# Two routed adapters on one core: weights fetched in one transfer and a step earlier, and two groups of weight factors moved in VectorE's order

## The chip, the cores and the metric

One core of one Trainium2 chip. The metric is the device time of one execution in microseconds (us); lower is better. Engines are named as in the profile: PE is TensorE, DVE VectorE, ACT ScalarE, POOL GpSimd, SP SyncE (here it only issues DMAs).

## The reference

128 items of 128 rows by 1024 columns pass two layers. Each layer is an adapter, and each item is routed to one of three sets of its weights (the drawn routes are 1 and 2, so two sets are used in each layer).

```
h = gelu(x @ W_down[route] + b_down[route])      # 1024 -> 512
y = x + h @ W_up[route] + b_up[route]            # 512 -> 1024
out = (y - mean) * rsqrt(var + 1e-5) * gamma[route] + beta[route]
```

Everything is fp32. The second layer takes the first one's output.

## The kernel before

**Order of the work.** The items are sorted on the chip by route and taken in pairs: 65 pairs for layer 0, 65 for layer 1, numbered 0 to 129. A pair takes one set of weights. Where the set of pair c differs from that of pair c-1, the flag `c_new[c]` is 1. It is 1 at the first pair and at three more, which the trace places at pairs 30, 65 (the change of layer) and 95. `c_near` marks new sets whose forerunner came one or two pairs before, `c_far` the others. All engines read these flags in branches written by `when` (load the flag from memory into a register, compare, jump over the body).

**Precision.** Each fp32 operand is split in a high part (ACT copies it to fp32r) and a low part (DVE subtracts the high one), and each product is three matmuls. So a new set of down weights costs ACT four copies (`high_wd`, L578) and DVE four subtractions (`low_wd`, L797), each of 128x1024. The up projection is done with seven products of blocks instead of eight, so a new set of up weights gives seven factors: three DVE operations form differences (`factors`, L822 to L826), a fourth follows (L835), and each of the seven factors takes an ACT copy (L593) and a DVE subtraction (`low_wu`, L816). Factors 0 to 3 are made in `take_wu_0`, 4 to 6 in `take_wu_2`.

**A step.** In step i PE does the down projection of pair i (two items, four quarters each, six matmuls per quarter, `down`, L506) interleaved with the seven products of pair i-3 (`product`, L518): 48 + 42 = 90 matmuls. The order is product 0, a quarter, product 1, a quarter, and so on, with the two last quarters after product 6. Products 0, 2, 4 and 6 go to a bank bX, 1, 3 and 5 to bZ. After a product DVE adds the bank to the rows in memory before PE may add to that bank again: `onto` (evictions 1 to 3, L901) and `last_onto` (4 to 7, L909). PE waits for eviction 3 before product 4 and for eviction 4 before product 5. ACT seeds the banks with biases (`seed_x` L651, `seed_z` L659), which must be there before product 0 and product 1 of the next step, and which wait for DVE's sign `s_cb`. `high_x`, `low_x` make the parts of the input, `high_h`, `low_h` (L674, L891) those of the hidden layer; `low_h(w, 0)` is the first group of them, `low_h(w, 1)` the second, and so on. In layer 1 DVE also transposes the input (L862), twice in a step. `square` (L684), `normal` (L692) on ACT, `scale` (L932) on DVE and `shift` (L452) on POOL are the layer norm.

**Order on DVE and ACT.** Each engine runs `end(i-1)`, then `begin(i)`, in that order, in loops of six steps; the jump back lies between `begin` of one step and its `end`. Those loops end their turns in steps 10, 16, 22 ... 58 and 75, 81 ... 123. On DVE `begin(i)` finishes with `low_h(w, 0)`, `take_wu_2` under its flag, the sign `s_wu[1]` that lets product 4 go, and `factors` under `c_near`. Then `end(i)` begins with eviction 3, the variance, two `scale`, `low_h(w, 1)` and eviction 4.

**Weights.** `fetch_down` asks for a set with eight DMAs of 256 KB, `fetch_up` likewise. For pair i+1 ACT issues `fetch_down` in `begin(i)` (`load_down`), half a step before the first use in `end(i)`; for the up weights two steps before. The first down weights and up weights are issued by SP.

## Time and profile before

| | |
|---|---|
| median of three runs | 2795.27 us (2795.16 to 2796.49) |
| time of the profiled execution | 2799.51 us |
| span of that execution, first to last instruction | 2797.6 us |
| granted TensorE clock, mean | 0.988 |
| PE / DVE / ACT / POOL busy | 96% / 74% / 60% / 49% of the span |
| DMA queue of SP / of ACT | 557.02 MB / 12.59 MB |

The busy time of PE counts matmuls whose ends are modelled and which overlap, so it isn't PE at its peak. The starts of matmuls are the better measure, and the rows below use them.

### The profile page before, as it was taken

How to read it: one execution, taken by the hardware profiler on the slowest of the kernel's cores; microseconds unless marked ns; L12 is line 12 of the kernel's file. 1: busy time of each engine (PE TensorE's matmuls, PEld its weight loads, DVE VectorE, ACT ScalarE, POOL GpSimd, SP SyncE). 2: the span in 40 equal slices, each digit the busy share in tenths (PEclk: the TensorE clock that was granted, in tenths of full speed). 3: DMA queues.
4: the chain of work that ended last, by engine and by line, in shares of the span. 5: the costliest groups of instructions: out<-in, count | busy, mean ns of one | idle time of the engine just before them, and what ended most of it. 6: DMA issues, size and time to landing. Idle time of an engine off the chain costs nothing.

```text
span 2797.6 us, 58384 instructions
## 1 busy us (share of the span) xinstructions
PE 2697.8 (96%) x11714; PEld 2209.0 (79%) x11714; DVE 2074.1 (74%) x3356; ACT 1676.1 (60%) x2905; POOL 1369.0 (49%) x1050
## 2 busy tenths in 40 slices
PE   7999999998999999999989999999889999999997
PEld 5788888877788888888768888888667888888885
DVE  5767677768777676777788777777787777877776
ACT  4565665655666656666556665656556656666564
POOL 1455555544455555555435444444434444544445
PEclk9999999999999999999999999999999999999999
DMA  7665566667565665656856665766766666666663
GB/s 197 202 214 201 204 212 199 212 208 219 192 210 199 214 203 201 213 204 208 240 184 222 200 212 188 223 197 219 206 205 208 205 207 201 209 198 218 203 202 146
DMA packets 366252, 574.00 MB, mean 205 GB/s; under 512 B 40992, under 2 KB 240800, under 8 KB 365728
## 3 DMA queue, kind: packets, MB, share of 16 engines
q1 hardware_dynamic: 360352, 557.02, 60.9%
q10 hardware_dynamic: 5376, 12.59, 1.9%
q14 instruction: 512, 4.19, 0.5%
q8 instruction: 12, 0.20, 0.0%
HBM read 364.97 MB, written 204.47 MB: 204 GB/s over the span
## 4 chain that ended last, share of the span: by engine, by line
PE 78%; issue 8%; DVE 7%; DVEq 2%; ACT 2%; DMA 1%; ACTq 1%; POOL 1%; SPq 0%; POOLq 0%
PE pD L506 41%; PE bX L518 21%; PE bZ L518 16%; DVEq L234 2%; DVE xt L909 1%; DVE hl L891 1%; DVE xt L932 1%; DMA rwd<-in_Wd 1%; DVE wul L816 1%; ACT xh L626 1%; ACTq L234 1%; DVE xT L862 0%; ACT pC L684 0%; DMA htok<-hg 0%; DVE xt L901 0%
## 5 line engine op out<-in xcount | busy, mean ns | idle before, releaser
L452 POOL TENSOR_TENSOR xt<-xt,cgb 128x1024 f32<-128x1024 f32 x258 | 621.1, 2408 | 455.3 <-ACT xt L692 455.3
L506 PE MATMUL pD<-wdh,xh 128*128 128x512 f32 x2080 | 814.1, 391 | 10.0 <-DVEq L853 9.6
L506 PE MATMUL pD<-wdl,xh 128*128 128x512 f32 x2080 | 812.1, 390 | 0.0
L506 PE MATMUL pD<-wdh,xl 128*128 128x512 f32 x2080 | 811.6, 390 | 0.0
L692 ACT ACTIVATE xt<-xt,rstd 128x1024 f32<-128x1024 f32 x258 | 296.1, 1148 | 297.0 <-POOL rstd L438 293.6
L506 PEld LDWEIGHTS pD<-wdh,xh 128*128 128x128 f32 x2080 | 392.7, 189 | 95.9 <-DVEq L853 8.4
L518 PE MATMUL bX<-wuh,hh 128*128 128x512 f32 x1040 | 411.0, 395 | 51.1 <-DVE xt L901 26.5
L684 ACT ACTIVATE pC<-xt,nmean 128x512 f32<-128x512 f32 x520 | 358.2, 689 | 169.0 <-DVE nmean L917 160.4
L506 PEld LDWEIGHTS pD<-wdl,xh 128*128 128x128 f32 x2080 | 392.9, 189 | 81.5
L506 PEld LDWEIGHTS pD<-wdh,xl 128*128 128x128 f32 x2080 | 392.3, 189 | 82.3
L674 ACT ACTIVATE hh<-cs 128x512 fp32r<-128x512 f32 x260 | 163.7, 630 | 465.3 <-PE bX L518 221.1
L518 PE MATMUL bX<-wul,hh 128*128 128x512 f32 x1040 | 408.1, 392 | 0.0
L518 PE MATMUL bX<-wuh,hl 128*128 128x512 f32 x1040 | 408.1, 392 | 0.0
L460 POOL TENSOR_TENSOR cs<-hT 128x256 f32<-128x256 f32 x130 | 96.9, 745 | 597.0 <-DVE hT L876 597.0
L435 POOL TENSOR_TENSOR rstd<-var,mhalf 128x2 f32<-128x2 f32 x129 | 215.3, 1669 | 348.8 <-DVE var L924 346.2
L891 DVE TENSOR_TENSOR hl<-cs,hh 128x512 fp32r<-128x512 f32 x260 | 191.0, 735 | 235.9 <-issue 208.4
L901 DVE TENSOR_TENSOR xt<-bX,xt 128x512 f32<-128x512 f32 x260 | 178.1, 685 | 240.9 <-PE bX L518 126.3
L518 PE MATMUL bZ<-wuh,hh 128*128 128x512 f32 x780 | 307.8, 395 | 21.0 <-DVE xt L909 16.1
L932 DVE SCALAR_TENSOR_TENSOR xt<-xt,nmean,cgb 128x1024 f32<-128x1024 f32 x260 | 321.8, 1278 | 0.6 <-POOLq L472 0.6
L518 PE MATMUL bZ<-wul,hh 128*128 128x512 f32 x780 | 304.7, 391 | 0.0
L518 PE MATMUL bZ<-wuh,hl 128*128 128x512 f32 x780 | 304.6, 391 | 0.0
L518 PEld LDWEIGHTS bX<-wuh,hh 128*128 128x128 f32 x1040 | 196.9, 189 | 100.9 <-DVE xt L901 33.7
(104 smaller groups left out, 3837.8 us busy)
## 6 DMA issues: line engine op xcount, KB each, us to landing
xq<-in_xB SPq DMA_DIRECT2D x130, 512.0 KB, 3.5
htok<-hg SPq DMA_DIRECT2D x260, 256.0 KB, 2.8
hq<-htok SPq DMA_DIRECT2D x1040, 64.0 KB, 2.2
xt<-in_x SPq DMA_DIRECT2D x130, 512.0 KB, 4.2
mid<-xt SPq DMA_DIRECT2D x130, 512.0 KB, 3.4
xq<-mid SPq DMA_DIRECT2D x520, 128.0 KB, 3.2
xt<-mid SPq DMA_DIRECT2D x130, 512.0 KB, 4.0
out<-xt SPq DMA_DIRECT2D x128, 512.0 KB, 2.9
```

The lines of the kernel that those rows point to most:

```text
L234: with eng.If(eng.value_load(flags[0:1, bass.ds(p.times(1), 1)], min_val=0, max_val=1) == 1):
L435: eng.tensor_tensor(rstd[:, n:n + 2], var[:, n:n + 2], mhalf[:, 0:1].broadcast_to([128, 2]), ALU.pow)\
L452: eng.tensor_tensor(xt[:, k, :], xt[:, k, :], cgb[:, 1, :], ALU.add).then_inc(s_o, 1)
L460: eng.tensor_tensor(cs[:, 0, :], b1, b2, ALU.add).then_inc(s_S, 1)
L506: last = eng.matmul(pD[e][:, :], a[:, e, 128 * k:128 * k + 128], w[:, k, :], start=False, stop=(k == 7 and n == 2), skip_group_check=True)
L518: last = eng.matmul(bank[:, :], a[:, left, 128 * c:128 * c + 128], w[:, n, c, :], start=(start and c == 0 and m == 0), stop=(c == 1 and m ...
L674: eng.activation(dst, src, ACT.Copy).then_inc(s_hh, 1)
L684: eng.activation(junk[:, :], xt[:, u.slot(e), K * m:K * m + K], ACT.Square, bias=nmean[:, n:n + 1], accum_out=ssq[:, b, m, e:e + 1]).then_ ...
L692: eng.activation(xt[:, k, :], xt[:, k, :], ACT.Copy, scale=rstd[:, n:n + 1]).then_inc(s_z, 1)
L891: eng.tensor_tensor(blocks, src, high.bitcast(fp32), ALU.subtract).then_inc(s_hl, 1)
L901: eng.tensor_tensor(half(u, e, m), bank[:, :], half(u, e, m), ALU.add).then_inc(s_v, 1)
L932: eng.scalar_tensor_tensor(out=xt[:, k, :], in0=xt[:, k, :], scalar=nmean[:, n:n + 1], in1=cgb[:, 0, :], op0=ALU.add, op1=ALU.mult).then_i ...
```

## The change

1. The host lays the weights out as they lie on chip, so that one partition's part is one contiguous run (16 KB). `fetch_down` and `fetch_up` are then one DMA of 2 MB each. Only the very first down weights come in four DMAs of 512 KB, one for each quarter, with a semaphore each.
2. The down weights are asked for one step further ahead: at a far new set in `begin` two steps before, at a near one as before. After `high_h(w, 0)` ACT then has five flagged branches in a step where it had four.
3. The first up weights are issued by ACT in `begin(0)` instead of by SP in its step 0.
4. On DVE `take_wu_2` (factors 4 to 6), its sign and the near `factors` branch move from ahead of eviction 3 to behind it.
5. On DVE `take_wu_0` (factors 0 to 3) and the signs `s_cb`, `s_wu[0]` move from ahead of eviction 6 to behind eviction 6 and `mean(u, 0, 6)`. In it the subtraction on the bias `cbu` (L837) moves from the end to the front.

```
         def fetch_down(eng, row, c):
             eng.wait_ge(f_rd, c + 1)
-            for h in range(2):
-                for a in range(4):
-                    r = 256 * a + 128 * h
-                    eng.dma_start(rwd[32 * a:32 * a + 32, 4 * h:4 * h + 4, :],
-                                  Wd[row, r:r + 128, :].rearrange("a (k i) n -> (a i) k n", i=32)).then_inc(s_rd[h], 16)
+            eng.dma_start(rwd[:, :, :].rearrange("p k n -> p (k n)"), Wd[row, :, :].rearrange("a p n -> (a p) n"))\
+               .then_inc(s_rd, 16)
...
# SP, before its steps
-            fetch_down(eng, row, 0)
+            eng.wait_ge(f_rd, 1)
+            for q in range(4):
+                eng.dma_start(rwd[:, 2 * q:2 * q + 2, :].rearrange("p k n -> p (k n)"),
+                              Wd[row, :, 2 * K * q:2 * K * q + 2 * K].rearrange("a p n -> (a p) n")).then_inc(s_rd0[q], 16)
...
# SP, step(i)
-                if i.first():
-                    fetch_up(eng, adapter(i), 0)
...
# ACT, begin(i)
                 high_h(i + -2, 0)
+                if i.first():
+                    fetch_up(eng, adapter(i), 0)
                 when_new(eng, i + -3, take_wu_2)
...
                 when(eng, c_near, i + -2, load_up)
                 when(eng, c_far, i, load_up)
-                when(eng, c_new, i + 1, load_down)
+                when(eng, c_near, i + 1, load_down)
+                when(eng, c_far, i + 2, load_down)
...
# DVE, take_wu_0
+                eng.wait_ge(s_bu, c * 16 + 16)
+                eng.tensor_tensor(cbu[:, K:H], cbu[:, K:H], cbu[:, 0:K], ALU.subtract).then_inc(s_bz, 1)
                 low_wu(c * 7, 0, b11)
...
                 eng.tensor_tensor(b11, t2, b11, ALU.subtract).then_inc(s_sub, 1)
-                eng.wait_ge(s_bu, c * 16 + 16)
-                eng.tensor_tensor(cbu[:, K:H], cbu[:, K:H], cbu[:, 0:K], ALU.subtract).then_inc(s_bz, 1)
...
# DVE, begin(i)
                 low_h(w, 0)
-                when_new(eng, u, take_wu_2)
-                ready(u, s_wu[1])
...
-                when(eng, c_near, w, factors)
...
# DVE, end(i)
                 onto(u, 3, X, 0, 1)
+                when_new(eng, u, take_wu_2)
+                ready(u, s_wu[1])
+                when(eng, c_near, w, factors)
...
                 low_x(i + 1, 0)
-                when(eng, c_new, w, take_wu_0)
-                ready(w, s_wu[0])
-                ready(w, s_cb)
                 last_onto(u, 6, bZ, 0, 0, 1)
                 mean(u, 0, 6)
+                when(eng, c_new, w, take_wu_0)
+                ready(w, s_cb)
+                ready(w, s_wu[0])
                 transpose_x(i + 1, 1)
```

## Rows read from the trace of the kernel before

**Rows 1.** The page's first part: busy time, share, instructions.

```profile
PE 2697.8 (96%) x11714; PEld 2209.0 (79%) x11714; DVE 2074.1 (74%) x3356; ACT 1676.1 (60%) x2905; POOL 1369.0 (49%) x1050
```

**Rows 2.** Timeline of PE (start, length, work, idle before): the starts of steps.

```profile
598.52 0.39 PE L518 MATMUL bX<-wuh,hh 128*128 128x512 f32 x1
...
627.51 0.80 PE L518 MATMUL bX<-wuh,hh 128*128 128x512 f32 x1 [2.56 <-ACT bX L651]
...
701.08 0.77 PE L518 MATMUL bX<-wuh,hh 128*128 128x512 f32 x1 [5.77 <-ACT bX L651]
...
750.00 0.39 PE L518 MATMUL bX<-wuh,hh 128*128 128x512 f32 x1
...
1364.24 0.40 PE L518 MATMUL bX<-wuh,hh 128*128 128x512 f32 x1
...
1465.79 0.39 PE L518 MATMUL bX<-wuh,hh 128*128 128x512 f32 x1
...
1979.70 0.39 PE L518 MATMUL bX<-wuh,hh 128*128 128x512 f32 x1
...
2005.54 0.47 PE L518 MATMUL bX<-wuh,hh 128*128 128x512 f32 x1 [0.85 <-issue]
...
2130.53 0.39 PE L518 MATMUL bX<-wuh,hh 128*128 128x512 f32 x1
```

**Rows 3.** Windows of the core: PE, PEld, DVE, ACT, POOL busy, clock, DMA.

```profile
616.20:620.50 4.30, 4.28 (x12) 3.36 (x13) 3.98 (x6) 1.63 (x3) 2.14 (x1) 0.60 1.03 227
...
1465.80:1588.20 122.40, 122.40 (x542) 101.39 (x541) 97.26 (x161) 76.50 (x136) 60.21 (x49) 1.00 0.67 219
```

**Rows 4.** Timeline of ACT and PE in step 29, ahead of pair 30.

```profile
607.78 6.24 ACTq L262 DMA_DIRECT2D rwd<-in_Wd  x8
...
616.23 0.50 PE L518 MATMUL bZ<-wuh,hh 128*128 128x512 f32 x1 [3.94 <-DVE xt L909]
...
623.40 2.01 ACT L578 ACTIVATE wdh<-rwd 128x1024 fp32r<-128x1024 f32 x2 [5.58 <-DMA rwd<-in_Wd]
```

**Rows 5.** Timeline of the start (ACT, SP, PE).

```profile
16.62 2.00 ACT L578 ACTIVATE wdh<-rwd 128x1024 fp32r<-128x1024 f32 x2 [1.00 <-DMA rwd<-in_Wd]
...
27.56 4.27 SPq L270 DMA_DIRECT2D rwu<-in_Wu  x8
...
51.17 0.50 PE L506 MATMUL pD<-wdh,xh 128*128 128x512 f32 x1 [2.53 <-DVEq L853]
```

**Rows 6.** Timeline of DVE: eviction 3 in steps 29 and 81.

```profile
606.50 0.69 DVE L901 TENSOR_TENSOR xt<-bX,xt 128x512 f32<-128x512 f32 x1 [1.47 <-issue]
...
1721.84 0.69 DVE L901 TENSOR_TENSOR xt<-bX,xt 128x512 f32<-128x512 f32 x1 [4.58 <-PE bZ L518]
```

**Rows 7.** Timeline of DVE and PE, layer 1: eviction 4, product 5 (steps 70, 81).

```profile
1517.26 0.68 DVE L909 SCALAR_TENSOR_TENSOR xt<-bZ,xt 128x512 f32<-128x512 f32 x1
...
1520.19 0.39 PE L518 MATMUL bZ<-wuh,hh 128*128 128x512 f32 x1
...
1726.26 0.50 PE L518 MATMUL bZ<-wuh,hh 128*128 128x512 f32 x1 [0.54 <-DVE xt L909]
```

**Rows 8.** Timeline of PE in step 67, behind `factors` of pair 65.

```profile
1414.84 0.50 PE L506 MATMUL pD<-wdh,xh 128*128 128x512 f32 x1 [1.48 <-DVEq L853]
```

**Rows 9.** Timeline of DVE in step 32: factors 0 to 3 of pair 30.

```profile
691.59 2.35 DVE L816 TENSOR_TENSOR wul<-rwu,wuh 128x1024 fp32r<-128x1024 f32 x2
...
696.13 3.36 DVE L835 TENSOR_TENSOR rwu<-twu,rwu 128x1024 f32<-128x1024 f32 x1
...
700.53 0.69 DVE L909 SCALAR_TENSOR_TENSOR xt<-bZ,xt 128x512 f32<-128x512 f32 x1 [0.43 <-DVE cbu L837]
```

**Rows 10.** Timeline of DVE and PE in step 33: factors 4 to 6 of pair 30, and eviction 3.

```profile
710.43 2.96 DVE L816 TENSOR_TENSOR wul<-rwu,wuh 128x1024 fp32r<-128x1024 f32 x2 [0.40 <-ACT wuh L593]
...
715.75 0.69 DVE L901 TENSOR_TENSOR xt<-bX,xt 128x512 f32<-128x512 f32 x1 [1.22 <-issue]
...
716.50 0.50 PE L518 MATMUL bX<-wuh,hh 128*128 128x512 f32 x1 [2.17 <-DVE xt L901]
```

More of the change, by code:

```diff
@@ L106, in routed_adapters @@
         c_first = sb("c_first", [1, 1], i32)
-        c_q = sb("c_q", [1, NPH + 1], i32)
+        c_q = sb("c_q", [1, NPH + 2], i32)
         c_new = sb("c_new", [1, NPH + 1], i32)
-        c_near = sb("c_near", [1, NPH], i32)
-        c_far = sb("c_far", [1, NPH], i32)
+        c_near = sb("c_near", [1, NPH + 2], i32)
+        c_far = sb("c_far", [1, NPH + 2], i32)
         rf, tf, kf, rq = (xt[:, 0, (NB + 1) * n:(NB + 1) * (n + 1)] for n in range(4))
@@ L132, in routed_adapters @@
             "s_it", "s_io", "s_id", "s_p", "s_first", "s_oh", "s_pc", "s_ctl", "s_far"))
-        s_rd = [sem(f"s_rd{k}") for k in range(2)]
+        s_rd0 = [sem(f"s_rd0{k}") for k in range(4)]
+        s_rd = sem("s_rd")
         s_ru = sem("s_ru")
@@ L258, in fetch_down @@
             eng.wait_ge(f_rd, c + 1)
-            for h in range(2):
-                for a in range(4):
-                    r = 256 * a + 128 * h
-                    eng.dma_start(rwd[32 * a:32 * a + 32, 4 * h:4 * h + 4, :],
-                                  Wd[row, r:r + 128, :].rearrange("a (k i) n -> (a i) k n", i=32)).then_inc(s_rd[h], 16)
+            eng.dma_start(rwd[:, :, :].rearrange("p k n -> p (k n)"), Wd[row, :, :].rearrange("a p n -> (a p) n"))\
+               .then_inc(s_rd, 16)
         def fetch_up(eng, row, c):
             eng.wait_ge(f_ru, c + 1)
-            for g in range(2):
-                for a in range(4):
-                    r = 128 * a + 64 * g
-                    eng.dma_start(rwu[32 * a:32 * a + 32, g, :, :, :].rearrange("p c n k -> p c (n k)"),
-                                  Wu[row, r:r + 64, :].rearrange("a (k i) n -> (a i) k n", i=32)).then_inc(s_ru, 16)
+            eng.dma_start(rwu[:, :, :, :, :].rearrange("p g c n k -> p (g c n k)"),
+                          Wu[row, :, :].rearrange("a p n -> (a p) n")).then_inc(s_ru, 16)
         b11, b12, b21, b22 = (rwu[:, g, :, n, :] for g in range(2) for n in range(2))
@@ L576, in high_wd @@
                 count(eng, s_Db, p + -1, 4, q + 1)
-                eng.wait_ge(s_rd[q // 2], c * 64 + 64)
+                if p.first():
+                    eng.wait_ge(s_rd0[q], 16)
+                else:
+                    eng.wait_ge(s_rd, c * 16)
                 eng.activation(wdh[:, 2 * q:2 * q + 2, :], rwd[:, 2 * q:2 * q + 2, :], ACT.Copy).then_inc(s_wdh, 1)
@@ L597, in take_wu_0 @@
                 count(eng, s_P, p + -1, 7, 4)
-                eng.wait_ge(s_ru, c * 128 + 128)
+                eng.wait_ge(s_ru, c * 16 + 16)
                 high_wu(0, b11)
@@ L784, in _ @@
             eng.memset(c_near[:, 0:1], 0)
+            eng.memset(c_near[:, NPH:NPH + 2], 0)
+            eng.memset(c_far[:, NPH:NPH + 2], 0)
             eng.tensor_tensor(c_near[:, 1:2], c_new[:, 1:2], c_new[:, 0:1], ALU.min)
@@ L1023 @@
         "itok": itok_B_1_2,
-        "Wd": np.concatenate([L0_cond_W_down, L1_cond_W_down]),
+        "Wd": np.concatenate([L0_cond_W_down, L1_cond_W_down]).reshape(6, 4, 8, 32, K).transpose(0, 1, 3, 2, 4)
+                .reshape(6, 128, 8 * K),
         "bd": np.concatenate([L0_cond_b_down, L1_cond_b_down]),
-        "Wu": np.concatenate([L0_cond_W_up, L1_cond_W_up]),
+        "Wu": np.concatenate([L0_cond_W_up, L1_cond_W_up]).reshape(6, 4, 4, 32, H).transpose(0, 1, 3, 2, 4)
+                .reshape(6, 128, 4 * H),
         "bu": np.concatenate([L0_cond_b_up, L1_cond_b_up]),
```

4 lines of the change are left out of this document (2 added, 2 removed).

## The prediction

> **What bounds the kernel now.** The page's first part comes first [rows 1]: PE is busy 96%, so the end is set by PE's stream wherever that runs, and a gain must come from its holes. How long a step is without one, a window shows: 122.40 us hold 542 matmuls, six steps of 90, so 20.40 a step at a clock of 1.00, the 2.4 GHz level [rows 3]. 130 such steps would be 2652; the span is 2797.6. Then the timeline of PE: the reader should lay step starts beside each other and take 20.40 off for each step between. Around pair 30 the six steps 29 to 34 take 151.48, 29.1 too much. Around pair 65 the four steps 65 to 68 take 101.55, 20.0 too much. Around pair 95 the six steps 94 to 99 take 150.83, 28.4 too much [rows 2]. That is 77.5 us at three new sets of weights. The rest is the start, the tail, and a hole of 0.2 to 1.4 us in most of the eighteen steps in which DVE's and ACT's loops turn; the last row of [rows 7] is one. In a plain step DVE, ACT and POOL lie beside PE, so an operation saved there gains nothing.
>
> **Part 1, weights in one DMA and a step ahead.** In step 29 eight DMAs hold ACT for 6.24; its `high_h(w, 1)` comes after them, DVE's eviction 4 behind that, and product 5 waits 3.94 [rows 4]. The pause costs clock too: from 616.20 to 620.50 the granted clock is 0.60, mostly the 1.2 GHz level [rows 3], and some nine matmuls come 0.2 late each. Then ACT waits 5.58 for the weights [rows 4], and step 30 starts 2.56 late for its bias seed [rows 2]. Step 29 lasts 28.99, 8.6 too much. Both waits go. The DMA now issued in step 28 costs ACT an eighth of 6.24, 0.8; nothing is queued there but `high_h(w, 1)`, which had some 1.4 to spare. With one more branch (0.9, below) that cover is just used up, and I leave 0.9 in steps 28 and 29: gain 7.7, bounds 6.5 and 8.6. Step 94 is the same case at 25.84, 5.4 too much [rows 2]; DVE enters step 95 with more in front of it (part 4), for which I give 0.8 back: gain 4.6, bounds 3 and 5.4. For pair 65 the weights arrive in time already; the up weights' eight DMAs on ACT delay an eviction slightly: gain 0.3. Steps 30, 65 and 95 stay long: four copies on ACT (two in 2.01 [rows 4]) and four subtractions on DVE lie ahead of eviction 1. The new wait for the buffer two steps ahead is long met at a far set.
>
> The Trainium skill, DMA: Bandwidth & Descriptors, section Queues, rings and completion order, says that each DMA engine alternates between queues a whole packet at a time, of up to 64 descriptors. By that rule rows of 16 KB could hold other transfers back behind much of the 2 MB. No row here has such a transfer; what it would do is rival (d), priced from rows.
>
> **Part 2, the start.** ACT waits 1.00 for half of the first weights [rows 5]. A first quarter lands sooner: gain 1.0, bounds 0 and 1.0. The first up weights are issued by SP for 4.27 from 27.56, and the `htok` and `hq` transfers run beside them; PE then waits 2.53 at 51.17, where DVE had to wait for `hq` [rows 5]. ACT can issue the one DMA at about 25, ahead of nothing that is due, and SP's queue loses eight, so the jam ends 3 to 6 earlier. I take this wait and 0.5 of a smaller one: gain 3.0, bounds 0 (the bytes are as slow) and 5.
>
> **Part 3, two branches behind eviction 3.** Between `low_h(w, 0)` (0.41) and eviction 3 the sequencer of DVE takes the two untaken branches: 0.41 + 1.47 idle [rows 6], some 0.9 a branch where no instruction runs over it. Behind eviction 3 (0.69) 0.6 of them is covered. In a plain step eviction 3 waits for PE anyway, so what follows it comes 1.15 later. The cover is the slack of eviction 4: in layer 1 it ends at 1517.94, product 5 goes at 1520.19 [rows 7], 2.25 to spare. So nothing is lost while the delay is below 2.25. In a turning step DVE is what PE waits for (4.58 idle for branches and the jump [rows 6]), and the 0.6 is a gain, capped by the hole. In layer 0 eight such steps give 3.8, step 34 another 0.6: gain 4.4, bounds 0 and 5.4.
>
> **Part 4, the third branch, in layer 1.** The `take_wu_0` branch is covered by `low_x` now. Behind the mean (0.2) some 0.75 of it is bare. In layer 0 DVE's waits for PE take that up. In layer 1 two transposes fill DVE: 1.15 and the bare branch, less what an eviction's wait gives, make 1.6 by the end of a step, and a wait of 0.5 ahead of eviction 2 leaves 1.1 at `low_h(w, 0)`. Less the 0.6 of part 3, nine turning steps have 0.5 more hole: loss 4.5, bounds 0 and 9.
>
> **Part 5, `factors`.** In steps 31, 66 and 96 it stands behind the same branch, and the sign for the next quarter of `down` stands behind it; in step 67 PE already waits 1.48 for that [rows 8], so every delay counts. 0.85, 1.3 and 1.3: loss 3.4, bounds 0 and 5.
>
> **Part 6, factors 0 to 3.** In step 32 DVE starts them at 691.59 and is at eviction 6 at 700.53, 3.36 of it in one subtraction [rows 9]; the seed of step 33 is late by 5.77 [rows 2]. Now they start behind product 5 (692.6), eviction 6 (0.69), the mean and a branch, at about 694.2: 2.6 later, and `s_cb` with them. The bias subtraction in front adds no wait, as the bias is asked for at that step's start; queued behind it are the four subtractions. In steps 67 and 97 DVE waited for ACT's copy anyway: 0.9 each. Loss 4.4, bounds 1 and 8.
>
> The Trainium skill, SBUF — State Buffer, section SBUF: two separate sides, has POOL and DVE shut each other out for a whole instruction where both read that memory and DVE has two inputs. The 3.36 agrees, as other subtractions take 1.2. By that rule the wait only moves to another subtraction; without it the sum would be some 6 lower.
>
> **Part 7, factors 4 to 6.** In step 33 three subtractions run from 710.43, then a branch, then eviction 3 at 715.75, for which PE waits 2.17 [rows 10]. Now eviction 3 goes at 710.3, a branch, the subtractions end at 715.3, and the second branch is hidden: 1.0 sooner. By the same count 0 in step 68, 0.7 in 98, 1.8 in step 3: gain 3.5, bounds 0 and 5.
>
> **Sum.** -7.7 - 4.6 - 0.3 - 1.0 - 3.0 - 4.4 - 3.5 + 4.5 + 3.4 + 4.4 = -12.2, and 0.3 back in step 65, whose DVE work starts later: -11.9. The profiled execution took 2799.51, 1.9 over its span and 4.2 over the median of the three runs; the difference is taken off the median: 2795.27 - 11.9 = 2783.4.
>
> **The rivals.** (a) The forecast, 2783.4: 0.46. With the parts' bounds (not all at one end) its own range is 2775 to 2790.
>
> (b) The moved work costs nothing. From 691 to 720 DVE is busy throughout, and its sum is the same in either order, so the 12.3 of losses go: 2795.3 - 24.2 = 2771, or 2775 with a third of them left. Against it: the bare branch. 0.16.
>
> (c) It doesn't do what it is made for. Steps 29 and 94 keep half of their 14.0, since DVE's and ACT's own work holds them: 2783.4 + 7 - 1 = 2789 or, with the start's 4.0 gone too, 2793. For it: the steps behind new down weights are long even at pair 65, where the weights come in time. Against it: the 3.94 and the 5.58 have one cause each. 0.15.
>
> (d) The 2 MB crowds SP's transfers. At the 219 to 227 GB/s of [rows 3] it lasts some 9 us; a `htok` store behind all of it eats the time until the transposes, and PE is held 2 to 4 at some of six fetches: 8 in all, 2791. For it: the wait at 51.17. Against it: the loads now start early in a step, ahead of the stores. 0.09.
>
> (e) Slower: eviction 4 in the plain steps of layer 1. It decides where DVE's delay passes 2.25. If the bare branches cost twice my 1.15, or the delay of part 4 isn't taken up by the waits and adds itself, some 55 plain steps grow; at 0.3 each that is 16.5, and 5 at the turns: 2805. For it: DVE has no other slack there. Against it: the 1.47. 0.14.
>
> **How the numbers follow.** A measurement of this kernel tells 0.2%, 5.6 us, from no change, so faster is below 2789.7. Of (a) 0.43 is faster, of (b) all, of (c) and (d) 0.05: 0.64. The same: the rest of (a), (c) and (d), 0.22. Slower: (e), 0.14. The range reaches from (b) to the far end of (c), 2771 to 2798; (e) and the tails lie outside.
>
> **What would show it.** Right: steps 29 and 94 within 1.5 of 20.40 and ACT's issue one DMA long; the seed of step 33 late by about 8; holes at turns smaller in layer 0, larger in layer 1. Wrong: plain steps over 20.40, a wait for `hq` or `htok` in steps 28 to 33, the seed's wait unchanged.

## The result, and the profile after

The changed kernel took 2833.28 us (2831.68 to 2837.71, four runs), the kernel before 2795.74 beside it. The ratio is 1.0137, 95% interval 1.0119 to 1.0154: slower by about 38, where 12 faster had been forecast.

The first part of the page, to be laid beside [rows 1]:

```profile
span 2835.8 us, 58851 instructions
PE 2713.0 (96%) x11714; PEld 2216.1 (78%) x11714; DVE 2084.8 (74%) x3358; ACT 1682.4 (59%) x2905; POOL 1348.3 (48%) x1050
```

The counts and the shares tell little: PE is again "busy 96%". Its busy time grew by 15.2 of the 38, because a matmul at a slower clock counts as busy for longer (0.63 in rows below, 0.39 in [rows 2]). The fourth part, the chain that ended last, says more. First the kernel before, then the changed one:

```profile
PE 78%; issue 8%; DVE 7%; DVEq 2%; ACT 2%; DMA 1%; ACTq 1%; POOL 1%; SPq 0%; POOLq 0%
```

```profile
issue 30%; PE 24%; DVE 19%; DVEq 11%; ACT 7%; POOL 6%; ACTq 2%; POOLq 1%; DMA 0%; SPq 0%
PE pD L503 12%; DVEq L236 10%; PE bX L515 7%; PE bZ L515 5%; DVE xt L914 5%; ACT xh L626 5%; DVE hl L896 4%; POOL rstd L432 2%; DVE xT L867 2%; DVE xt L937 2%; POOL cs L459 2%; ACT pC L684 1%; DVE xt L906 1%; ACTq L236 1%; DVE wul L821 1%
```

The chain ran through PE before; now it runs through DVE and its sequencer. L236 is the branch in `when`: 10% of the span on DVE's queue, where its line in the chain of the kernel before (L234) had 2%.

**Where the 38 came.** The sum over steps, each from its first matmul of product 0 to the next step's (worked out from the timeline of PE; a step without a hole is 20.40; the stretch 130 to 132 ends with the start of the last matmul). "Turning" are the steps in which DVE's and ACT's loops turn and no new set lies near: 10, 16, 22, 40, 46, 52, 58 and 75, 81, 87, 105, 111, 117, 123. The other columns are experiments, told below.

| stretch (steps) | before | after | e1 | e13 | e3 | e4 | e5 | e9 | e12 | e10 | e14 |
|---|---|---|---|---|---|---|---|---|---|---|---|
| start of step 4 | 85.6 | 77.8 | 81.0 | 78.4 | 83.7 | 84.4 | 85.4 | 85.6 | 85.7 | 77.6 | 76.3 |
| turning, layer 0 (7) | 147.3 | 156.9 | 148.5 | 146.3 | 147.2 | 163.0 | 150.7 | 173.7 | 156.0 | 147.2 | 144.8 |
| turning, layer 1 (7) | 148.7 | 167.9 | 150.1 | 154.4 | 152.9 | 161.9 | 156.7 | 171.5 | 162.8 | 149.5 | 144.3 |
| 28 to 34 | 172.6 | 176.5 | 167.7 | 169.6 | 172.1 | 176.9 | 174.2 | 181.6 | 177.7 | 166.8 | 163.4 |
| 64 to 68 | 122.0 | 124.3 | 120.7 | 122.6 | 125.7 | 125.9 | 124.9 | 132.1 | 124.3 | 121.2 | 119.9 |
| 93 to 99 | 172.1 | 175.9 | 171.3 | 177.0 | 173.2 | 176.9 | 174.7 | 182.6 | 180.2 | 170.9 | 164.9 |
| 130 to 132 | 41.6 | 45.7 | 40.9 | 43.0 | 43.7 | 42.9 | 41.1 | 42.8 | 40.3 | 41.5 | 40.5 |
| others, layer 0 (46) | 938.4 | 940.6 | 938.4 | 938.4 | 938.4 | 946.8 | 938.4 | 959.6 | 939.2 | 938.4 | 938.4 |
| others, layer 1 (47) | 958.8 | 959.5 | 958.8 | 958.8 | 958.8 | 963.2 | 959.0 | 990.3 | 962.1 | 958.8 | 958.8 |

From before to after: -7.8 at the start, +9.6 and +19.2 at the turning steps, +3.9, +2.3 and +3.8 around the three new sets, +4.1 in the tail, +2.9 in all others: 38.0, and the spans differ by 38.2. Three quarters of the loss lie in fourteen steps that have nothing to do with weights.

**A turning step in layer 1.** Step 81 starts at 1724.97. Timeline of DVE; eviction 3 (L906, 1734.81) answers to [rows 6], eviction 4 (the last row) to [rows 7]:

```profile
1722.83 1.26 DVE L867 STREAM_TRANSPOSE xT<-xq 128x1024 f32<-128x1024 f32 x1 [1.26 <-issue]
1725.25 0.69 DVE L896 TENSOR_TENSOR hl<-cs,hh 128x512 fp32r<-128x512 f32 x1 [1.16 <-issue]
...
1731.33 0.84 DVE L896 TENSOR_TENSOR hl<-hT,hh 128x256 fp32r<-128x256 f32 x1
1734.81 0.69 DVE L906 TENSOR_TENSOR xt<-bX,xt 128x512 f32<-128x512 f32 x1 [2.64 <-PE bZ L515]
1736.86 0.16 DVE L929 SCALAR_TENSOR_TENSOR var<-ssq 128x2 f32<-128x2 f32 x1 [1.36 <-issue]
...
1740.10 0.68 DVE L914 SCALAR_TENSOR_TENSOR xt<-bZ,xt 128x512 f32<-128x512 f32 x1
```

of DVE in the kernel before, where step 81 starts at 1711.96:

```profile
1710.15 0.69 DVE L891 TENSOR_TENSOR hl<-cs,hh 128x512 fp32r<-128x512 f32 x1 [1.31 <-issue]
...
1725.52 0.68 DVE L909 SCALAR_TENSOR_TENSOR xt<-bZ,xt 128x512 f32<-128x512 f32 x1
```

and of PE after, product 5, which goes with eviction 4:

```profile
1740.83 0.58 PE L515 MATMUL bZ<-wuh,hh 128*128 128x512 f32 x1 [1.91 <-DVE xt L914]
...
1742.07 0.63 PE L515 MATMUL bZ<-wuh,hh 128*128 128x512 f32 x1
1742.50 0.63 PE L515 MATMUL bZ<-wul,hh 128*128 128x512 f32 x1
```

The reader is to see the delay being handed on. The first half of the step begins with `low_h(u, 2)` (L896) at 1725.25, 0.28 behind the step's start; in the kernel before it was at 1710.15, 1.81 ahead of it. `low_h(w, 0)` follows at 1731.33, the loop turns with no branch beside it, and eviction 3 runs at T+9.84 (T being the step's start), as early as before. But then come two branches, 1.36 bare ahead of `var`, and eviction 4 runs at T+15.13. In the kernel before it was at T+13.6. PE waits 1.91 instead of the 0.54 of [rows 7].

The rows of eviction 3 name "PE bZ", product 3, as what ended its idle time, here and in [rows 6]. By the code it waits for product 2 alone, and where it runs before product 3 has ended (T+9.24 in the kernel before, step 16) the profile names "issue". So the 4.58 of [rows 6] is indeed DVE's sequencer, as the prediction read it.

What comes behind PE's wait is slow. Windows of the changed kernel (as [rows 3]): ahead of the wait, behind it, and, for comparison, behind the wait of step 87, which is 1.91 as well:

```profile
1728.00:1735.40 7.40, 7.40 (x34) 6.12 (x33) 4.66 (x7) 2.95 (x6) 2.89 (x4) 1.00 0.54 160
1740.80:1744.50 3.70, 3.67 (x9) 2.90 (x10) 3.12 (x5) 2.44 (x4) 1.59 (x1) 0.54 0.30 120
...
1867.40:1871.10 3.70, 3.70 (x16) 3.08 (x17) 3.11 (x5) 2.47 (x4) 1.57 (x1) 1.00 0.31 123
```

Behind the pause of 0.54 the kernel before kept a clock of 1.00. Behind that of 1.91 in step 81 it is 0.54, nearly all at the 1.2 GHz level, with matmuls 0.43 apart (the last two rows above) instead of some 0.23. That is why 1.4 more of waiting makes the step 3.2 longer (21.23 and 24.41). It doesn't follow each such wait: of layer 1's seven turning steps, all with waits of 1.91 to 1.94, five lose clock and take 24.3 to 24.5, while two (87 and 105) keep it and take 23.0. In layer 0 one of seven loses it (step 16). These runs don't show what decides it. I had counted this multiplier in step 29 and nowhere else.

**Layer 0.** Step 22, the same picture with the end of the other branch. Timeline of DVE, after:

```profile
451.42 0.69 DVE L896 TENSOR_TENSOR hl<-cs,hh 128x512 fp32r<-128x512 f32 x1 [3.43 <-issue]
...
462.44 0.16 DVE L929 SCALAR_TENSOR_TENSOR var<-ssq 128x2 f32<-128x2 f32 x1 [1.37 <-issue]
```

and before:

```profile
451.65 0.69 DVE L891 TENSOR_TENSOR hl<-cs,hh 128x512 fp32r<-128x512 f32 x1 [2.15 <-issue]
```

Three branches behind the mean hold the sequencer for 3.43; two held it for 2.15. Over 43 plain steps of layer 0 (between 5 and 61) the median pause from the mean's end to this `hl` was 2.42 before and 3.83 after: **1.4 for the branch that I had put at 0.75**, with two signs, which e6 below puts at 0.1. In layer 1 this branch alone lies between the mean and the next transpose: nothing is idle there before, and the median over 42 plain steps is 1.27 after. The waits of the whole run say it in totals, the kernel before first:

```profile
DVE hl L891 <- issue: 208.4, 119, 2.5
ACT bX L651 <- DVEq L853: 17.3, 4, 5.0
PE bZ L518 <- DVE xt L909: 16.1, 20, 3.9
```

```profile
DVE hl L896 <- issue: 269.5, 120, 4.5
ACT bX L651 <- DVEq L858: 210.4, 127, 6.1
DVE var L929 <- issue: 137.6, 128, 1.4
PE bZ L515 <- DVE xt L914: 41.7, 21, 4.9
```

The second line is a sign raised late, not by itself a loss: ScalarE's bias seed now waits for DVE's sequencer in 127 steps instead of 4.

**The weights.** What the change was made for worked: step 29 took 28.99 before and 20.40 after, step 94 25.84 and 20.40. But the step in front grew: step 28 from 21.08 to 27.22, step 93 from 21.25 to 27.81, and so did the step behind, 30 from 26.69 to 28.85, 95 from 27.46 to 29.13. The three steps 28 to 30 took 76.75 before and 76.47 after, 93 to 95 took 74.54 and 77.34: nothing was gained in all. Timeline of ACT and PE in step 28, after, answering to [rows 4]:

```profile
585.02 0.35 ACTq L261 DMA_DIRECT2D rwd<-in_Wd  x1
592.03 0.63 ACT L674 ACTIVATE hh<-cs 128x512 fp32r<-128x512 f32 x1 [10.84 <-issue]
...
594.05 0.67 PE L515 MATMUL bZ<-wuh,hh 128*128 128x512 f32 x1 [4.94 <-DVE xt L914]
```

The DMA is 0.35 long, as I had said. `high_h(w, 1)` runs 7.01 behind it all the same: step 28 is one in which ACT's loop turns, and the taken branch stands right ahead of the turn. PE then waits 4.94 in that step for the eviction behind it.

**The factors.** Timeline of DVE in steps 32 and 33 and of PE in step 33, after, answering to [rows 9, 10]:

```profile
692.79 0.69 DVE L836 TENSOR_TENSOR cbu<-cbu 128x512 f32<-128x512 f32 x1 [1.19 <-issue]
...
695.67 3.36 DVE L821 TENSOR_TENSOR wul<-twu,wuh 128x1024 fp32r<-128x1024 f32 x1
...
700.09 1.21 DVE L842 TENSOR_TENSOR rwu<-twu,rwu 128x1024 f32<-128x1024 f32 x1
...
711.00 0.69 DVE L906 TENSOR_TENSOR xt<-bX,xt 128x512 f32<-128x512 f32 x1 [1.51 <-PE bX L515]
...
715.63 0.47 PE L515 MATMUL bX<-wuh,hh 128*128 128x512 f32 x1 [0.59 <-DVEq L858]
...
720.34 0.50 PE L515 MATMUL bZ<-wuh,hh 128*128 128x512 f32 x1 [1.74 <-DVE xt L914]
```

and of PE in step 33 of the kernel before, product 5, behind the product 4 of [rows 10]:

```profile
720.17 0.50 PE L518 MATMUL bZ<-wuh,hh 128*128 128x512 f32 x1 [0.61 <-DVE xt L909]
```

Eviction 3 of step 33 waits for PE alone again, and the 3.36, which stood in another subtraction [rows 9], is found in a low part instead, while the old one takes 1.21. That the wait only moves is what the prediction drew from the Trainium skill, SBUF — State Buffer, section SBUF: two separate sides; the trace agrees with its number. Product 4 comes 1.0 sooner in its step (T+14.38, before T+15.42), but the three subtractions now stand ahead of eviction 4, and product 5 waits 1.74 instead of 0.61: both kernels have it at T+19.09, and step 33 takes 26.02 in both. Step 32 takes 26.49 before and 29.03 after. The seed of step 33 came 6.47 late instead of 5.77, and PE waits 1.44 for the sign behind `factors`, for which it didn't wait before.

### The profile page after: what moved, and what is told of

Read it like the earlier page. It is cut to its first block, busy times and chain, and to the rows that moved or that the text cites. A ratio compares the mean times of both kernels' runs of the same rounds, so it can differ in the third digit from the quotient of the medians.

```text
span 2835.8 us, 58851 instructions
## 1 busy us (share of the span) xinstructions
PE 2713.0 (96%) x11714; PEld 2216.1 (78%) x11714; DVE 2084.8 (74%) x3358; ACT 1682.4 (59%) x2905; POOL 1348.3 (48%) x1050
## 3 DMA queue, kind: packets, MB, share of 16 engines
q14 instruction: 467, 3.83, 0.5%
## 4 chain that ended last, share of the span: by engine, by line
issue 30%; PE 24%; DVE 19%; DVEq 11%; ACT 7%; POOL 6%; ACTq 2%; POOLq 1%; DMA 0%; SPq 0%
PE pD L503 12%; DVEq L236 10%; PE bX L515 7%; PE bZ L515 5%; DVE xt L914 5%; ACT xh L626 5%; DVE hl L896 4%; POOL rstd L432 2%; DVE xT L867 2%; DVE xt L937 2%; POOL cs L459 2%; ACT pC L684 1%; DVE xt L906 1%; ACTq L236 1%; DVE wul L821 1%
## 5 line engine op out<-in xcount | busy, mean ns | idle before, releaser
L449 POOL TENSOR_TENSOR xt<-xt,cgb 128x1024 f32<-128x1024 f32 x258 | 629.6, 2441 | 433.9 <-ACT xt L692 433.9
L896 DVE TENSOR_TENSOR hl<-cs,hh 128x512 fp32r<-128x512 f32 x260 | 179.3, 690 | 295.8 <-issue 269.5
L432 POOL TENSOR_TENSOR rstd<-var,mhalf 128x2 f32<-128x2 f32 x129 | 186.0, 1442 | 281.3 <-DVE var L929 281.3
L874 DVE TENSOR_TENSOR xl<-xq,xh 128x1024 fp32r<-128x1024 f32 x130 | 234.8, 1806 | 39.3 <-ACT xh L626 33.2
```

The lines of the kernel that those rows point to most:

```text
L432: eng.tensor_tensor(rstd[:, n:n + 2], var[:, n:n + 2], mhalf[:, 0:1].broadcast_to([128, 2]), ALU.pow)\
L449: eng.tensor_tensor(xt[:, k, :], xt[:, k, :], cgb[:, 1, :], ALU.add).then_inc(s_o, 1)
L874: eng.tensor_tensor(xl[:, e, :], src, xh[:, e, :].bitcast(fp32), ALU.subtract).then_inc(s_xl, 1)
L896: eng.tensor_tensor(blocks, src, high.bitcast(fp32), ALU.subtract).then_inc(s_hl, 1)
```

## The experiments

Fourteen runs, in four groups that each had the kernel before on the same chip.

| run | median, us | range | ratio to before | 95% interval |
|---|---|---|---|---|
| e1 | 2789.25 | 2786.15 to 2792.43 | 0.9972 | 0.9959 to 0.9984 |
| e2 | 2847.76 | 2845.82 to 2854.3 | 1.0175 | 1.0158 to 1.0192 |
| e3 | 2810.05 | 2806.68 to 2811.77 | 1.0043 | 1.0026 to 1.006 |
| e4 | 2856.05 | 2853.5 to 2862.31 | 1.0214 | 1.0194 to 1.0233 |
| e5 | 2819.2 | 2817.52 to 2819.91 | 1.0082 | 1.0065 to 1.0098 |
| e9 | 2933.18 | 2927.53 to 2934.29 | 1.0484 | 1.0466 to 1.0501 |
| e6 | 2799.49 | 2797.41 to 2802.13 | 1.0008 | 0.9999 to 1.0018 |
| e7 | 2784.98 | 2784.07 to 2786.77 | 0.9958 | 0.9944 to 0.9972 |
| e8 | 2785.58 | 2782.88 to 2789.75 | 0.9961 | 0.9947 to 0.9974 |
| e10 | 2784.75 | 2783.78 to 2787.17 | 0.996 | 0.9944 to 0.9975 |
| e11 | 2791.53 | 2787.6 to 2794.29 | 0.998 | 0.9971 to 0.9989 |
| e12 | 2843.98 | 2840.92 to 2846.67 | 1.0173 | 1.0157 to 1.0188 |
| e13 | 2802.92 | 2800.14 to 2807.52 | 1.0025 | 1.0016 to 1.0035 |
| e14 | 2766.31 | 2763.81 to 2769.91 | 0.99 | 0.9884 to 0.9917 |

### Which half of the change: VectorE's order, or the rest

**e1**, the changed kernel with VectorE's order of before (both moves below undone):

```
             low_h(w, 0)
+            when_new(eng, u, take_wu_2)
+            ready(u, s_wu[1])
...
+            when(eng, c_near, w, factors)
...
             onto(u, 3, X, 0, 1)
-            when_new(eng, u, take_wu_2)
-            ready(u, s_wu[1])
-            when(eng, c_near, w, factors)
...
             low_x(i + 1, 0)
+            when(eng, c_new, w, take_wu_0)
+            ready(w, s_wu[0])
+            ready(w, s_cb)
             last_onto(u, 6, bZ, 0, 0, 1)
             mean(u, 0, 6)
-            when(eng, c_new, w, take_wu_0)
-            ready(w, s_cb)
-            ready(w, s_wu[0])
```

> The changed kernel with VectorE's order of before (factors 0 to 3 ahead of eviction 6, factors 4 to 6 ahead of eviction 3, the bias subtraction last); weights in one DMA, a step ahead, as changed. Theory A, untaken branches that no DVE instruction runs over make DVE late, so that PE waits for eviction 4 in the turning steps and its clock falls: those steps go back to about 21.2 us, the start's gain of 7.8 stays, and the time is about 2786 (2780 to 2791). Theory B, ACT's fifth branch in a step and its loads make high_h(w, 1) late: the turning steps stay at 22 to 24.4, about 2825. Theory C, the 2 MB transfers hold up others: 2825 or more too, with waits on hq or xq.

Measured 2789.25, with turning steps of 21.2 and 21.4, as theory A had it; the start kept 4.6 of the 7.8. The order alone turns a gain of 8 into a loss of 38. ScalarE's added branch and the wide transfers are still in this kernel, so neither costs that much by itself.

**e2**, the kernel before with both moves (the diff above with its signs turned round, and the bias subtraction ahead of the four low parts in `take_wu_0`) and nothing else; **e3**, with the two branches behind eviction 3 alone; **e4**, with the branch of `take_wu_0`, its signs and the bias subtraction behind the mean alone.

> The kernel before with both of VectorE's moves and nothing else. Theory A: all the loss of the turning steps is here, 29 us, with 4 in the tail and 5 to 10 around the new sets, so 2830 (2822 to 2840). Theories B and C: within 5 us of before, 2791 to 2801.

> The kernel before with factors 4 to 6 and the near-factors branch behind eviction 3, and nothing else. Theory A: the two branches now cost 1.35 behind eviction 3, which plain steps absorb; in a turning step they are partly covered; -3 to +4 in all, 2796 (2791 to 2801). If the number of branches between eviction 3 and eviction 4 is what counts by itself, PE waits some 1.3 us more in 18 turning steps: 2819 or more.

> The kernel before with factors 0 to 3 behind eviction 6 and the mean, the bias subtraction first, and nothing else. Theory A: one bare branch of 1.2, which reaches low_h(w, 0) with 0.5 to 0.7 left and is paid in 18 turning steps (some 11), in three factor steps (3.6) and at the seeds of three new sets (4): 2813 (2805 to 2822). If this move is harmless: within 3 us of before.

Measured: 2847.76, 2810.05 and 2856.05, each above theory A's range (e3 lies between its two accounts). That the loss lies in VectorE's order alone was right, and every size was too low: e3 costs 13, where about nothing was expected, e4 59, both together 51. In e4 DVE reaches `low_h(u, 2)` of step 22 0.77 behind the step's start, `hl` waiting 3.44 for issue, and is late for eviction 3 (T+12.3, before T+10.3) and eviction 4 alike; putting the other two branches behind eviction 3 takes part of that back, so the terms don't add.

**e13**, the changed kernel with only the second of the two moves undone.

> The changed kernel with the branch of take_wu_0, its signs and the bias subtraction back in their old order ahead of eviction 6; the two branches behind eviction 3 stay there. Theory A (the bare branch behind the mean is most of the loss, the two behind eviction 3 little, 13 us on the kernel before): 2789 plus 13, 2802, between 2796 and 2809. Rival N (in the changed kernel the two behind eviction 3 are what holds eviction 4, and cost at least as much): 2812 to 2830.

Measured 2802.92, where 2802 was expected. So in the changed kernel itself the branch behind the mean carries 30 of the 44 that lie between e1 and the changed kernel, and the two behind eviction 3 carry 14. Rival N, which had it the other way round, falls.

### Is it the branch, or what moved with it

**e5** and **e9**, the kernel before with one or two more branches behind the mean, never taken:

```
             mean(u, 0, 6)
+            when(eng, c_near, w, lambda p: eng.sem_inc(s_seen, 1))
             transpose_x(i + 1, 1)
```

(e9 has the added line twice.) **e6** leaves the branch where it was and raises its two signs later:

```
             low_x(i + 1, 0)
             when(eng, c_new, w, take_wu_0)
-            ready(w, s_wu[0])
-            ready(w, s_cb)
             last_onto(u, 6, bZ, 0, 0, 1)
             mean(u, 0, 6)
+            ready(w, s_cb)
+            ready(w, s_wu[0])
```

> The kernel before with one more branch on VectorE behind the mean of eviction 6, on a flag that is never set here; nothing else is changed and the branch for the factors stays where it was, ahead of eviction 6. Theory A (the price is in the bare branch itself, about 1.2 us of VectorE's time in every step, which the turning steps cannot absorb): some 50 us slower, as where that branch alone was moved there (2856): 2850, between 2825 and 2870, with eviction 3 and eviction 4 both later in the turning steps. Theory F (the price of the moved branch was in the factors and signs that came later with it, not in the branch): 2797 to 2806.

> The kernel before with two such branches on VectorE behind the mean of eviction 6, on a flag that is never set here. Theory A: the delay doubles, and every microsecond of it beyond the slack of the evictions lengthens a step: at least twice the loss of one such branch, 2880 to 2960, with plain steps of layer 1 over 20.40 as well. Theory F: 2798 to 2815.

> The kernel before with the two signs that the factors and the bias are ready raised behind eviction 6 and the mean; the branch itself stays ahead of eviction 6. Theory A: the signs' place alone matters little, since the branch stays covered: 2798, between 2794 and 2808. Theory F (ScalarE's bias seed waits for the sign in nearly every step, and that is what cost the time): 2830 or more.

Measured: 2819.2, 2933.18 and 2799.49. A branch that does nothing costs 22, two cost 136. The signs' 2 can't be told from nothing (0.9999 to 1.0018). Theory F falls (e6), and A holds in kind: the second branch costs five times the first. The pause from the mean to `hl` tells why. Its median over the same 43 plain steps is 2.42 before, 3.19 with one and 4.21 with two, 0.9 for each; with one it is ScalarE's `hh` that ends the pause in 42 of the 43 steps, with two it is the sequencer in all 43. The first branch mostly fills slack, the second has none left: the "others" of layer 1 in the table go from 959.0 to 990.3, which one branch didn't touch. e5 came out below its range (2825 to 2870): I had expected the loss of e4, 59.

**e12** has the long body of `take_wu_0` behind that never-taken branch instead of one sign:

```
             mean(u, 0, 6)
+            when(eng, c_near, w, take_wu_0)
             transpose_x(i + 1, 1)
```

> The kernel before with one more branch on VectorE behind the mean of eviction 6, on a flag that is never set, as in the run with one such branch, but with the long body of take_wu_0 in it instead of one sign. Theory K (a branch not taken is a jump over its body, and costs more over a long one: 1.3 us instead of 0.9): between the runs with one and with two short ones (2819 and 2933), 2840 to 2875, with VectorE's pause from the mean to its next instruction 0.4 above that of the run with one. Rival L (the body's length is nothing; the difference lies in the signs behind the moved branch): 2815 to 2824.

Measured 2843.98, 25 above e5, with not one instruction of the body executed. Rival L falls by the time, and the time is in theory K's range. But K's mechanism, 0.4 more at the branch itself, isn't there. In layer 0 the median pause is 3.20, against 3.19 in e5; ScalarE ends it in 41 steps, so VectorE's sequencer was ready no later than that. In layer 1, where the added branch alone lies between the mean and the transpose and nothing else is waited for, the median over 42 plain steps is 1.24, against 1.17. Timeline of DVE in step 81 (T is 1720.34 in e5, 1731.23 in e12), e5 first; the transpose is the first row:

```profile
1717.23 1.26 DVE L862 STREAM_TRANSPOSE xT<-xq 128x1024 f32<-128x1024 f32 x1 [1.18 <-issue]
1719.22 0.69 DVE L891 TENSOR_TENSOR hl<-cs,hh 128x512 fp32r<-128x512 f32 x1 [0.73 <-ACT hh L674]
```

```profile
1728.88 1.26 DVE L862 STREAM_TRANSPOSE xT<-xq 128x1024 f32<-128x1024 f32 x1 [1.05 <-issue]
1730.88 0.69 DVE L891 TENSOR_TENSOR hl<-cs,hh 128x512 fp32r<-128x512 f32 x1 [0.74 <-issue]
```

`hl` lies 1.12 ahead of the step in e5, 0.35 ahead in e12, though the pauses are no longer. Part of the delay arises ahead of them: in plain steps of layer 1 a median idle time of 0.23 stands ahead of eviction 6, behind the older branch over the same body, where e5 has none. By which path the added code costs time, these runs don't show.

The Trainium skill, Runtime: NRT & Kernel Launch, section Instruction fetch mechanics, has an engine stall at a taken branch whose target lies outside the two pages of code that it holds. The jump over a long body could be such a branch, but the pauses at it show no stall. The profile does count transfers of instructions, without the engine that they are for. In the third part of the page, e5 and then e12:

```profile
q14 instruction: 513, 4.20, 0.5%
q14 instruction: 533, 4.37, 0.5%
```

The long body brings 20 more. In the kernel before a turning step of layer 1 has 8 or 9 of these packets and the steps beside it 2 to 4. That code has to be fetched anew at each turn is a reading that fits both; no run tested it.

**e14** takes a branch away. It is e10 (below) without VectorE's branch for the factors on a near flag, which stood between `low_h(w, 0)` and the loop's turn and is never taken here; where sets follow each other closely the kernel would leave that work out.

```
                 if i.j is None and i.c == 2:
                     take_wu_0(Pair(0))
-                when(eng, c_near, w, factors)
```

> The run without the step ahead (VectorE's old order, one DMA each, new start: 2784.8), and on VectorE without the branch for factors on near flags, which stands bare between low_h(w, 0) and the turn of the loop and is never taken here; the kernel would leave that work out where sets follow each other closely. Theory A (the holes of the turning steps are VectorE's bare branches and its jump; one branch fewer frees 0.9 to 1.2 in each): layer 0's seven turning steps from 147.2 to 143 to 144.5, layer 1's from 149.5 to 143.5 to 146, 2777 in all, between 2772 and 2781. Rival M (ScalarE's turn sets them as well, so VectorE's relief shows little): 2782 to 2787.

Measured 2766.31, 18 below e10 and beyond A's range on the good side. The body goes with its branch, so this doesn't tell which of them is worth it. Layer 0's turning steps fell to 144.8 (143 to 144.5 expected), layer 1's to 144.3 as expected; most of the rest of the gain is in the stretches around the new sets (3.4, 1.3 and 6.0), where I had counted none. Where DVE sets the pace, a branch less is worth 0.3 to 0.9 a step, by stretch. Timeline of DVE, eviction 3 in step 81 (T is 1697.12 in e10, 1687.66 in e14), e10 first:

```profile
1707.29 0.69 DVE L905 TENSOR_TENSOR xt<-bX,xt 128x512 f32<-128x512 f32 x1 [4.87 <-PE bZ L515]
```

```profile
1696.90 0.69 DVE L905 TENSOR_TENSOR xt<-bX,xt 128x512 f32<-128x512 f32 x1 [3.94 <-issue]
```

Eviction 3 comes 0.93 sooner in its step (T+10.17, T+9.24). Even with that branch gone, one branch and the jump cost 3.94 of DVE's time in a turning step.

### What the weights' part is worth

**e10** is e1 without the step ahead, **e11** is e10 with the old start too (the first down weights in one DMA, the first up weights issued by SP). **e7** and **e8** are e1 with the load moved away from ScalarE's loop turn:

```
e10, in begin(i):
-                when(eng, c_near, i + 1, load_down)
-                when(eng, c_far, i + 2, load_down)
+                when(eng, c_new, i + 1, load_down)
e7, in begin(i), and in end(i):
-                when(eng, c_far, i + 2, load_down)
...
                 seed_z(w)
+                when(eng, c_far, i + 2, load_down)
e8, in begin(i):
-                when(eng, c_near, i + 1, load_down)
-                when(eng, c_far, i + 2, load_down)
+                when(eng, c_far, i + 3, load_down)
```

> The changed kernel with VectorE's old order, and with the next down weights asked for one step ahead as before; they still come in one DMA. Theory A (two causes in steps 29 and 94: ACT's eight issues, and the weights' late landing): the landing's part comes back, ScalarE waits some 4 us for the weights in step 29, and step 28 loses its 2.3: against 2789 about 2791, between 2786 and 2796. Rival H (the eight issues alone cost it, or the wide rows land so much sooner that the step ahead buys nothing): 2785 or less, with steps 28 and 29 together at 41.5 to 43.

> As the run without the step ahead, and the start put back too: the first down weights in one DMA, the first up weights issued by SP. Left of the change are the host's layout and one DMA each. Theory A (the start's gain comes from where the first up weights are issued and from the quarters): 3 to 4 slower than the run without the step ahead, start of step 4 back at 84 to 86. Rival J (the layout makes the start's gain): within 1.5 of that run, start of step 4 at 79 to 82.

> The changed kernel with VectorE's old order, and with ScalarE's load of the next down weights (its branch with it) taken from the end of a step's first half, where the next instructions are the loop's turn, to behind the seeds of bX and bZ. Theory A (the taken branch beside the loop's turn holds ScalarE for 6.9 us in steps 28 and 93, which cost 2.3 and 4.0 more than a plain turning step): against 2789 for the same kernel with the load in its place 2783, between 2779 and 2786, with steps 28 and 93 at 21.0 to 21.7. Rival G (a taken branch with a DMA costs that wherever it stands, or the 2 MB itself does it): 2787 to 2792, with steps 28 and 93 at 23 and 25 as there, or 27 to 29 and 92 to 94 longer in their stead.

> The changed kernel with VectorE's old order, the next down weights asked for three steps ahead instead of two, and without the branch on ScalarE that asks for them one step ahead (its flag is never set here; the kernel would leave out that load where sets follow each other closely). The load then falls in steps 27, 62 and 92, none of which is one in which the loop turns. Theory A (a taken branch costs ScalarE some 6 us, which a plain step hides at that place and a turning step does not): against 2789 with the load in steps 28 and 93 and 2785 with it later in these steps: 2779, between 2775 and 2783, with steps 27 to 29 and 92 to 94 all within 1.3 of 20.40. Rival G (the branch costs the same in a plain step, or the 2 MB itself does it): 2785 to 2790, with steps 27 and 92 at 22 or more.

Measured: e10 2784.75, e11 2791.53, e7 2784.98, e8 2785.58.

e10 is not slower than e1: asking a step ahead as the change does it buys nothing that these runs can tell. Its step 29 takes 21.88 with the weights still landing late. Timeline of ACT, e10 and then e11, whose code in this step is the same:

```profile
600.23 0.36 ACTq L261 DMA_DIRECT2D rwd<-in_Wd  x1
600.77 0.63 ACT L674 ACTIVATE hh<-cs 128x512 fp32r<-128x512 f32 x1 [3.99 <-PE bZ L515]
...
608.79 2.01 ACT L578 ACTIVATE wdh<-rwd 128x1024 fp32r<-128x1024 f32 x2 [3.47 <-DMA rwd<-in_Wd]
```

```profile
602.99 1.69 ACTq L261 DMA_DIRECT2D rwd<-in_Wd  x1
...
615.29 2.00 ACT L574 ACTIVATE wdh<-rwd 128x1024 fp32r<-128x1024 f32 x2 [6.79 <-DMA rwd<-in_Wd]
```

In e10 one issue in place of eight brings `high_h(w, 1)` from 15.69 behind the step's start, in the kernel before, to 9.75, and step 29 from 28.99 to 21.88: 7.1 of its 8.6. What is left for the weights' late landing (the wait of 3.47) is 1.5 there, and 2.9 in step 94 (23.27). In the profiled execution of e11 ScalarE waits 6.79 for the weights and step 29 takes 25.64. PE has no wait for eviction 4 in either, as it had in the kernel before. So the eight issues are worth between 3.3 and 7.1 in this step, and the late landing between 1.5 and 5.2, by the execution. Both accounts hold in part: A's wait of some 4 for the weights is there, and the time (2784.75) and the sum of steps 28 and 29 (43.04) lie at rival H's.

e1, e7 and e8 say why the step ahead doesn't collect even that. Sums of steps 28 and 29, and of 93 and 94, from the timeline of PE: before 50.07 and 47.09; e1 43.74 and 45.63; e7 44.41 and 45.41; e8 41.57 and 42.96; e10 43.04 and 44.82. With the step behind, 28 to 30 and 93 to 95: before 76.75 and 74.54; e1 71.64 and 74.62; e7 70.84 and 69.88; e8 69.87 and 71.39; e10 71.03 and 73.02. In e8 the load falls into steps 27 and 92, where the loop doesn't turn, and both take 20.40 and 20.41. Timeline of ACT in e1, step 28, and in e8, step 27:

```profile
580.86 0.35 ACTq L261 DMA_DIRECT2D rwd<-in_Wd  x1
587.80 0.63 ACT L674 ACTIVATE hh<-cs 128x512 fp32r<-128x512 f32 x1 [10.75 <-issue]
```

```profile
559.86 0.35 ACTq L261 DMA_DIRECT2D rwd<-in_Wd  x1
560.40 0.63 ACT L674 ACTIVATE hh<-cs 128x512 fp32r<-128x512 f32 x1 [3.85 <-PE bX L515]
```

The same taken branch with the same DMA: the next instruction runs 6.94 behind the issue where the loop turns, 0.54 where it doesn't. The turn itself is part of the 6.94, and e8 has one branch fewer on ScalarE; the fair comparison is e1's own step 22, with the same five branches, none taken, and the turn: 6.55 idle ahead of `high_h(w, 1)`, where step 28 has 10.75. So taking the branch beside the turn costs 4.2. Theory A's mechanism holds for e8 in nearly all the steps that it named (93, at 21.86, is 1.5 above 20.40), and rival G's steps (27 and 92 at 22 or more) did not appear; but the time, 2785.58, lies in G's range and not in A's. I had counted 10 for those steps, and they gave 4.8 in the profiled runs (43.74 to 41.57 and 45.63 to 42.96). In e7, whose time is in A's range, the branch stands behind the seeds, steps 28 and 93 are as short as forecast (20.72, 21.61), and steps 29 and 94 rise to 23.69 and 23.80: at that place the cost came back, half as rival G had it.

e11 was to tell the start apart. In its profiled execution, with the layout and one DMA each but the old places, step 4 starts at 80.4; in the eight kernels with the old start that was 83.7 to 85.7, and in the seven with the full new start 76.3 to 81.0 (e1 and e7, with the same code there, 80.95 and 77.34). So rival J has that figure. But the times speak against it: e11 is 6.8 slower than e10 where J had at most 1.5, and none of its ten times (2787.6 at best) reaches one of e10's four (2787.17 at worst). The profiled execution was e11's fastest, 3.9 below its median. Neither account fits: of e10's 12.3 the layout and one DMA each bring 5.5, and the quarters and the move of the first up weights to ScalarE 6.8, more than the 3 to 4 of theory A. Where those 6.8 lie, the profile of the fastest execution doesn't show.

## Why the prediction was wrong

The time, the sign and the range were wrong; rival (e) had the sign, at 0.14, with the wrong place.

- **The step that failed is part 4**, "some 0.75 of it is bare" and "in layer 0 DVE's waits for PE take that up": a loss of 4.5, bounds 0 and 9. Measured, 30 (the changed kernel against e13) to 59 (e4). The branch's own price was 1.3 to 1.4 and not 0.75: I had worked it out from the pause of 1.47 for two branches [rows 6], and the longer pauses behind the mean (2.15 for two, in step 22 above) would have given 1.1 to 1.2. The second sentence failed too: layer 0's seven turning steps went from 146.3 in e13 to 156.9, beside 154.4 to 167.9 in layer 1. Behind the branch DVE has one wait for PE in them, ahead of eviction 2, 0.86 in the median of the kernel before. But part 3's branches had used it up: in e13, where DVE comes 1.2 later, it is nothing, and so the whole of the branch arrives at eviction 3 (median T+7.92 in e13, T+9.16 after) and eviction 4 (T+13.21, T+14.48). In layer 0 each part was weighed against the slack of the kernel before, as if the other had left it there.
- **Part 3** forecast a gain of 4.4. Layer 0's turning steps did gain 2.2 (148.5 in e1, 146.3 in e13), layer 1's lost 4.3, and with 28 to 34, 64 to 68, 93 to 99 and the tail the two branches behind eviction 3 cost 14. I weighed the slack of eviction 4 in a plain step, 2.25, and it was there: the plain steps stayed at 20.40. I didn't ask for that slack in a turning step, where [rows 7] has it at -0.54.
- **The clock** multiplied the wait in six of the fourteen turning steps: 1.00 ahead of it, 0.54 behind it, in step 81.
- **Part 1**: the mechanism was half right. The eight issues were a cause in step 29 (7.1 of 8.6 by e10, 3.3 by e11). "The DMA now issued in step 28 costs ACT an eighth of 6.24, 0.8" failed: 4.2 at a turn (e1's steps 28 and 22) with the old order on VectorE, and with the new order PE waited 4.94. A forecast of 12.6 for the two sets came out as 7.8 in e1 (6.3 and 1.5), of which 2.7 is lost again in steps 30 and 95; e8 got 12.6 (8.5 and 4.1) in those four steps, and gave 2.6 back there.
- **Part 2**: 4.0 forecast. Step 4 starts 4.6 to 9.3 earlier in the kernels with the new start; by the medians the quarters and the new place alone bring 6.8 (e10 against e11). The way was right, and the size, bounds 0 and 6, if anything too small.
- **Part 5** was about right: for the sign behind `factors` PE waits 1.44, 1.50 and 1.39 in steps 32, 67 and 97 of the changed kernel, 4.3 in all, where the kernel before had 1.48 and 0.39 in the last two and e1 nothing; forecast 3.4.
- **Part 6** didn't come: the seeds of steps 33, 68 and 98 came 6.47, 6.28 and 6.00 late, where the kernel before had 5.77, 6.48 and 6.43. I had looked for about 8 in the first.
- **Part 7** had the 1.0 for product 4 of step 33 right, but stopped there: product 5 lost it again, waiting for eviction 4.
- **Rivals.** (b), that moved work is free, is refuted by the 44 between e1 and the changed kernel; its "from 691 to 720 DVE is busy throughout" overlooks 2.08 of idle time by "issue" at 703.55, the branches themselves. (d), that the transfers crowd SP's, is refuted at its price by e1, which has all the transfers and is faster. (c) has a core of truth: steps 29 and 94 fell to 20.40, but the steps around them took it back. (e) set the point "if the bare branches cost twice my 1.15": the two behind eviction 3 cost 1.36, the one behind the mean 1.3 more, and the plain steps of layer 1 still stayed within 0.7 in all. It takes one branch more (e9, +31.5 there) to reach them.

Left open: by what path the code of a branch's body costs time, what decides whether the clock falls behind a wait of 1.9, and how the 2.9 in the changed kernel's other steps arise, most of them in layer 0 a few steps behind a turn (12, 13, 37 to 39); no run aimed at these.

## What to carry to other kernels

An untaken branch on an engine's queue is an instruction of 0.8 to 1.4 us that no list of busy times shows: count the branches between two dependent instructions as work, and price the step where the engine has the least slack, not the step that occurs most often. Where two moves lean on the same slack, count it once. A flagged branch belongs behind a long instruction or ahead of one that waits anyway, not beside the loop's turn; one branch less, with its body, gave more here (18 us) than the weights' new layout, issue and start together (12, e10). And a wait that grows from half a microsecond to two costs its length and, in six of fourteen steps here, a slower clock behind it.
